# Splitting the B and C rows later, and a dense tile's gates, experts and residual a section sooner

## The reference

```python
x_ = einsum('ed,bld->bel', in_proj_w, ctx); u = silu(conv4(x_) + conv_b)
dt_lo, Bm, Cm = split(einsum('ke,bel->bkl', x_proj_w, u))          # 32, 16, 16 rows
delta = softplus(einsum('er,brl->bel', dt_proj_w, dt_lo) + dt_proj_b)
state = state * exp(delta_t * A) + (delta_t * u_t) * B_t           # per state, over time
y = (sum over states of state * C_t + D * u) * silu(z)             # z = layernorm(x)
x = x + y
```

```python
xn = layernorm(x); logits = xn @ W_router.T; h = xn @ A_w
x = x + xn @ W_base.T + b_base + sum over top-2 e of gate_e * 2 * (h_e @ B_w[e])
```

## Time and profile before

| | us |
|---|---|
| median of 3 runs (lowest, highest) | 2019.85 (2019.84, 2026.95) |
| the profiled execution, its own time | 2023.09 |
| its span | 2021.3 |
| PE, DVE, POOL, ACT busy | 1808.8, 1744.8, 1681.3, 1290.0 |
| share of PE, DVE, POOL, ACT | 89%, 86%, 83%, 64% |
| DMA | 435.01 MB, mean 215 GB/s |

### The profile page before, as it was taken

One profiled execution on the slowest core, in us unless ns is written; L12 is line 12 of the kernel. 1 busy time (PEld: TensorE's weight loads), 2 busy tenths in 40 slices (PEclk: granted clock), 3 DMA queues, 4 the chain that ended last, 5 costly groups with the idle time before them and its releaser, 6 DMA issues.

```text
span 2021.3 us, 25834 instructions
## 1 busy us (share of the span) xinstructions
PE 1808.8 (89%) x9000; PEld 1171.5 (58%) x9000; DVE 1744.8 (86%) x1397; ACT 1290.0 (64%) x1800; POOL 1681.3 (83%) x751
## 2 busy tenths in 40 slices
PE   8778888888788889899988899898999999989999
PEld 3346666666455555555555555565666666665554
DVE  3699999988999999999999999999999999995111
ACT  3485666666666676766676766666877777773332
POOL 0298999999998999999999999999999999997100
PEclk9889999998889999899999999999999999999999
DMA  4656666687786667697766676686676767666100
GB/s 160 213 199 211 218 209 205 211 298 268 240 283 215 217 201 223 219 311 256 250 221 218 205 230 212 213 299 224 233 226 225 227 227 224 226 228 246 57 31 32
DMA packets 158705, 435.01 MB, mean 215 GB/s; under 512 B 14608, under 2 KB 47632, under 8 KB 158576
## 3 DMA queue, kind: packets, MB, share of 16 engines
q1 hardware_dynamic: 155120, 420.79, 61.4%
q0 software_dynamic: 3456, 12.58, 3.2%
HBM read 382.46 MB, written 50.86 MB: 214 GB/s over the span
## 4 chain that ended last, share of the span: by engine, by line
DVE 38%; PE 31%; issue 15%; POOL 8%; ACT 6%; DMA 1%; DVEq 0%; POOLq 0%; SPq 0%; ACTq 0%
DVE state L1277 24%; DVE row L1259 9%; PE bank_a L642 6%; PE y_ps L586 6%; POOL prod L1419 5%; DVE conv L1251 3%; PE bank_b L642 3%; PE row L664 3%; POOL drive_rows L1412 2%; ACT decay L980 2%; PE row L580 2%; PE row L543 1%; PE bank_b L519 1%; PE bank_b L500 1%; ACT row L980 1%
## 5 line engine op out<-in xcount | busy, mean ns | idle before, releaser
L1419 POOL TENSOR_TENSOR prod<-state,c_rows 128x1024 f32<-128x1024 f32 x512 | 1209.5, 2393 | 101.1 <-PE y_ps L586 50.1
L1277 DVE TENSOR_TENSOR_SCAN state<-decay,row 128x1024 f32<-128x1024 f32 x355 | 808.8, 2283 | 21.0 <-PE row L580 13.5
L586 PEld LDWEIGHTS y_ps<-ident,prod 128*128 128x128 f32 x4096 | 488.0, 146 | 245.8 <-issue 158.7
L586 PE MATMUL y_ps<-ident,prod 128*128 128x128 f32 x4096 | 552.0, 282 | 46.2 <-POOL prod L1419 46.1
L642 PE MATMUL bank_a<-w_o,xnT 128*128 128x512 f32 x816 | 388.1, 606 | 12.3 <-DVE x L1324 12.3
L980 ACT ACTIVATE decay<-delta,a 128x1024 f32<-128x1024 f32 x355 | 397.3, 1137 | 1.5 <-DMA u_d<-decay 1.4
L1412 POOL TENSOR_TENSOR drive_rows<-du,b_rows 128x1024 f32<-128x1024 f32 x157 | 376.5, 2398 | 6.9 <-DMA b_rows<-bc_d 6.9
L1259 DVE TENSOR_TENSOR row<-du,row 128x1024 f32<-128x1024 f32 x296 | 358.1, 1210 | 25.1 <-PE row L543 24.8
L1277 DVE TENSOR_TENSOR_SCAN state<-row,drive_rows 128x1024 f32<-128x1024 f32 x157 | 357.3, 2276 | 19.3 <-POOL drive_rows L1412 15.5
L980 ACT ACTIVATE row<-delta,a 128x1024 f32<-128x1024 f32 x157 | 175.4, 1117 | 261.3 <-DVE state L1277 260.8
L543 PE MATMUL row<-parts,sel 96*128 96x512 bf16 x592 | 189.6, 403 | 80.7 <-DVE state L1277 74.3
(11 more groups left out here) (160 smaller groups left out, 1879.3 us busy)
## 6 DMA issues: line engine op xcount, KB each, us to landing
c_rows<-bc_d SPq DMA_DIRECT2D x512, 512.0 KB, 4.6
xrow<-in_x SPq DMA_DIRECT2D x32, 512.0 KB, 5.3
skip<-u_d SPq DMA_DIRECT2D x32, 512.0 KB, 8.8
yy_d<-yy SPq DMA_DIRECT2D x32, 512.0 KB, 6.5
u_d<-conv SPq DMA_DIRECT2D x24, 512.0 KB, 5.3
ctx<-u_d SPq DMA_DIRECT2D x48, 256.0 KB, 6.2
x<-in_x SPq DMA_DIRECT2D x24, 512.0 KB, 5.8
x<-yy_d POOLq DMA_DIRECT2D x24, 512.0 KB, 9.5
```

Source lines behind the costliest of these rows:

```text
L586: last = nc.tensor.matmul(y_ps[:, i * P:(i + 1) * P], source[:, i * P:(i + 1) * P], ident[:, :], start=(first and i % (H // P) == 0), stop ...
L1277: nc.vector.tensor_tensor_scan(state[:, q % STATES, :], factor, term, 0.0, ALU.mult, ALU.add).then_inc(scan_done, 1)
L1419: nc.gpsimd.tensor_tensor(prod[:, q % PRODS, :], state[:, q % STATES, :], c_rows[:, q % RING, :], ALU.mult).then_inc(prod_ready, 1)
```

## The change

Five things are edited. On PE `turn_gates` goes from section 11 to the end of section 10 (behind `add_up`), the experts of half 0 from section 12 to section 11, and half 1 of the product begins in section 12: in blocks without a third half two steps k in each of sections 12 to 15, in blocks with one none, three, two and three. On ACT `take_gates` goes from section 11, behind both table loads, to section 10, ahead of them. On DVE the residual of half 0 goes from section 13 to 12. On ACT the second split goes from section 7 to 9 and the third from 10 to 13. On POOL the second subtraction goes from section 8 to 10. No instruction is added or removed.

```diff
--- before.py
+++ after.py
@@ -758,15 +758,14 @@
                         k = 2 * at.index(m)
                         product(j, 0, [k, k + 1], beside, True)
                     if m == 11:
-                        turn_gates(j, beside, True)
-                    if m == 12:
                         experts(j, 0, beside)
                 for i, at in enumerate(front_plan(E)[0]):
                     if m in at and len(HALVES[E]) > i and m >= 9:
                         project(E, i, [k for k in range(NK) if at[k % len(at)] == m])
                 if dense:
-                    if m >= 13:
-                        product(j, 1, range(2 * (m - 13), NE if m == 15 else 2 * (m - 13) + 2), beside, True)
+                    if m >= 12:
+                        ks = ((), (0, 1, 2), (3, 4), (5, 6, 7)) if len(HALVES[E]) > 2 else ((0, 1), (2, 3), (4, 5), (6, 7))
+                        product(j, 1, ks[m - 12], beside, True)
                     if m == 15:
                         experts(j, 1, beside)
 
@@ -776,6 +775,8 @@
                     add_up(q - 2)
                 if m == 6:
                     add_skip(E)
+                if dense and m == 10:
+                    turn_gates(j, beside, True)
 
                 if m == 15 and E + 1 < NBLK and ON_PE[E + 1]:
                     turn_du(E + 1, 0)
@@ -1139,7 +1140,7 @@
                     take_gate(E, gate_at(E).index(m - 1))
                 if last and m - 1 in sizes_at(E):
                     take_v(E + 1, sizes_at(E).index(m - 1))
-                if last and m == 7:
+                if last and m == 9:
                     split_second(b + 1)
                 if dense and m == 5:
                     take_routing(j, beside)
@@ -1152,8 +1153,10 @@
                         gate_scale(E + 1)
                 if r == NE - 2 and b + 1 < B and m == 9:
                     take_xd(b + 1, 0)
-                if last and m == 10:
+                if last and m == 13:
                     split_third(b + 1)
+                if dense and m == 10:
+                    take_gates(j, beside)
 
                 if E + 1 < NBLK:
                     if m == 10:
@@ -1162,8 +1165,6 @@
                     if m == 11:
                         table(SILU)
                         gate_rows(E + 1)
-                if dense and m == 11:
-                    take_gates(j, beside)
                 if (E, m) in DIAGONALS_AT:
                     make_diagonal(*DIAGONALS_AT[E, m], range(NE))
                 if E == 0 and m >= FIRST_PIECE:
@@ -1367,7 +1368,7 @@
                     else:
                         dve.wait_ge(gate_copied, 2 * E + 2)
                     gates(j, beside)
-                if dense and m == 13:
+                if dense and m == 12:
                     add_residual(j, 0, beside)
                 scan(E, m)
                 if m == 2 and E:
@@ -1454,7 +1455,7 @@
                 product(E * DS + m)
                 if j >= -1 and m == 6:
                     add_yy(j + 1, E if r == 0 else E - 1)
-                if r == NE - 1 and b + 1 < B and m in (6, 8):
+                if r == NE - 1 and b + 1 < B and m in (6, 10):
                     split_rest_of(b + 1, m == 6)
                 if m == 12 and E + 1 < NBLK:
                     make_du(E + 1)
```

## The result

The forecast was 2013.2 us, 6.7 us (0.33%) under the median then shown. Measured side by side on one chip, the changed kernel takes 2030.26 us (median of 20 runs, 2023.5 to 2041.51), the kernel before 2023.3 (20 runs, 2018.73 to 2028.24). The ratio is 1.0037, 95% interval 1.0026 to 1.0049: 7.5 us slower, between 5.3 and 9.9. The direction was wrong, and by 14 us in all. (Against the 2013.2 the median lies 17 us off; 3.5 of that is the starting point, a median of three runs that twenty runs put at 2023.3.) The profiled execution took 2029.47 us, span 2027.7 (before: 2023.09 and 2021.3). The lengths of blocks (first scan to first scan) split these 6.4 us: up to the end of block 8 it is 3.4 us shorter (3.3 of it by the end of block 6, ahead of every edit, so not by the change); blocks 9 to 23 are 5.0 us longer, blocks 24 to 31 4.8 us.

What follows compares the result with a forecast made beforehand. VectorE and GpSimd, both nine tenths busy, were taken as the bound, gains lasting only if GpSimd follows. 6.7 + 2.7 - 0.7 - 2.0 = 6.7 us off 2019.85 gave 2013.2 us; range 2008 to 2021.5.

Steps and rivals of the forecast that it cites:

- part 5: TensorE leaves section 15 sooner, idles ahead of section 2's gate transposes, clock falls in five blocks: costs 2.0 us, bounds 0 to 5.
- The slower rival: TensorE's clock falls in blocks 24 to 31 behind idle time grown from 1.14 to 1.5 us: 3 us slower, 2023; chance 0.08.
- parts 2 and 3: Experts and third half moved in blocks with a third half; ScalarE's gates' copy ahead of its table loads: each valued at 0.
- Part 1: Half 1 begins a section sooner, so waits at ends of blocks 10, 13, 21 and for the residual go: 6.7 us gained.
- Part 4: Later splits and subtraction: 2.7 us gained at block 23's end, 0.7 lost in block 7, nothing in block 15.
- The rival in which nothing is removed: The residual still waits and TensorE's idle time stays: part 1 is 0, sum near 0, 2020; 0.26 shared with gains given back.
- The one with more than forecast: VectorE truly the bound in block 23 and the half-speed stretch never comes: 12.9 us gained, 2007; chance 0.14.

Runs made afterwards that it cites:

- e3: Changed kernel with half 1 of the dense product back in sections 13 to 15, earlier gates and experts kept; 1.0011 of the kernel before (2023.9 us).
- e12: Changed kernel with one matmul whose result nobody reads in section 1 of blocks 24 to 31 alone; 1.0002 of the kernel before (2024.33 us).
- e5: Kernel before plus unread filler matmuls in section 1: two in blocks 10 to 23, one in 24 to 31; ratio 0.997 (2016.74 us).
- e6: Changed kernel with the same filler matmuls as e4, but the splits at their old places; 0.9927 of the kernel before (2008.21 us).
- e4: Changed kernel plus unread filler matmuls in section 1: two in blocks 10 to 23, one in 24 to 31; 0.9927 of the kernel before (2009.03 us).
- e9: Changed kernel with half 1 back in sections 13 to 15 and the filler matmuls of e4; 0.9982 of the kernel before (2020.36 us).
- e1: Kernel before with the later splits alone (second split, third split, second subtraction); ratio 1.0011 (2026.42 us).
- e2: Changed kernel with the splits put back to their old places, no filler; 1.0031 of the kernel before (2031.89 us).
- e10: e4 with two more filler matmuls in sections 0 and 1 of block 9, splits later only in block 23; 0.992 of the kernel before (2006.91 us).
- e11: Changed kernel with filler matmuls only in blocks 11, 14, 16, 19, 22 (two) and 24 to 31 (one); 0.9991 of the kernel before (2020.2 us).

## Why the prediction was wrong

**The step that failed is part 5, the term of 2.0 us.** The mechanism was the right one and stands in the text: TensorE leaves section 15 sooner, waits longer ahead of the gate's transposes, and its clock falls. The size was wrong. After the change `drive` waits 23.0 us; before, 20.6 less the 7.8 at the four ends and 3.5 of block 23 left 9.3. So the term is 13.7 us, with 2.0 taken and 5 as its upper end; with the filler 6.4 us of waits remain. Three readings made it small:
- The price of a fall was had by dividing 9.3 us over all 15 blocks, and a block was to pay 1.0 at most. But before the change only seven blocks had a fall in section 2 or 3, with waits of 5.2 us behind it, up to 1.5 in a block; the rest of the 9.3 stands at other places. Now the five blocks counted (11, 14, 16, 19 and 22) pay 7.8 us more, 1.6 each; block 11 pays 0.79 + 1.03.
- Only those five were counted. In the seven others the idle time grew as well (2.75 and 2.50 to 2.89), and in some of them the half speed now lasts through the 16 instructions of section 3's `add_up` (3.62 us in place of 2.12 in block 12). They pay 6.0 us more: block 12's waits went from 1.19 to 2.26 us, block 18's from 0.38 to 1.90, block 21's at these places from none to 1.86.
- Blocks 24 to 31 were left at zero in the sum; the profile shows 4.8 us there.

Stretch by stretch the profile's miss of 13.1 us (6.7 sooner forecast, 6.4 later measured) is this: blocks 9 to 23 were to be 7.4 us shorter and are 5.0 longer, the rest behind them was to stay and is 4.8 longer, and ahead of them 0.7 longer was forecast and 3.4 shorter came, nearly all of it ahead of any edit, which is chance.

**The slower rival named the second place, with its chance far too low.** I gave it 0.08, since the idle time would grow from 1.14 to 1.5 us. It grew to 2.2: of the two us by which section 15 is lighter one comes back as idle time here, and I had argued only a third of a microsecond without working it out. Section 15 is not the whole of it either: with half 1 put back (e3) the gap is still 1.78, so 0.6 of the growth comes with the earlier gates and experts, whose parts 2 and 3 were put at nothing; by which of them is not shown. Per fall it costs 3.3 us and 0.6 in the next block, not 1.8, in block 28; but it comes in two blocks of seven, not in all, and the one in block 31 cost next to nothing. By e12 it is worth some 7 us on the median, with intervals that just touch.

The Trainium skill (TensorE: Matmul & The Clock Gate, section "Why this matters for your kernels") asks only to avoid idle gaps above about 3 us. In this trace the clock fell behind gaps of 2.0 to 2.9 us in a dozen blocks, and those falls decided the sign of the change; where the two differ the measurement decides.

**Part 1 was right in kind and, with the filler in place, too small:** 6.7 forecast, 8.7 (e5 to e6) or 11 (e4 to e9) measured. The stall after 2.81 us of idle time is gone, and with it every wait of `drive` at section 15; a part of the gain is in the next block's sections 1 and 2 (e9). Without the filler it is all given back, and more.

**Parts 2 and 3 were right for VectorE,** apart from the idle time of TensorE said above: outside block 23 no wait of VectorE for ScalarE's decay came up in sections 13 and 14, and blocks 25 to 27 are still 51.05 to 51.08 us.

**Part 4, forecast +2.0, is near 0** (e1: 1.0011; e4 against e6 the same). In block 23 the cover that goes is GpSimd's, as said, but the stall behind it grew from 1.25 to 4.67 us, so less is kept than the 2.7. Block 15 was put at nothing, since the subtraction would fill the wait for the C row. It did, but the product behind it starts 0.8 us later, and GpSimd has no gap up to block 16: VectorE's waits for it there are 2.88 and 1.66 in place of 0.42, against 2.86 saved. From its first scan to the second of the next block, block 7 takes 58.26 us in e2 and 58.99 in the changed kernel, block 15 60.24 and 61.48, block 23 61.74 and 60.09: +0.7 as forecast, +1.2 for 0, and -1.7 for -2.7. Between the kernel before and e1 the same three differ by -0.1, +0.3 and -1.7, so the two costs depend on when the C rows land, and the medians tell no gain.

The rival in which nothing is removed is excluded (block 13's rows). The one with more than forecast had said 2007, and e4, e6 and e10 come to 2007 to 2009 where half speed is rare. That is near by luck: its sum has 6.9 us from block 23, where VectorE still waits 4.66 us in e4, and the filler is no part of the change and gains 6 us without it.

## What to carry to other kernels

When a change makes a nearly full engine's section lighter, follow where that engine waits next: time comes back as idle time there (here one to two us for two), and if TensorE's clock falls behind it, what follows costs more than the section saved. Price such a fall per block that has one, never as a mean over all, and count it in every block whose idle time grows. A few matmuls that nobody reads, put into the gap, are a cheap test of whether a kernel's loss is the clock's, and here they turned a loss of 0.4% into a gain of 0.7%.

## What the runs showed of the hardware

- The clock falls behind gaps of 2.0 us here, and not each time: in blocks 25 to 31 of the changed kernel seven gaps of 2.2 to 2.7 us are followed by two falls, in e3 six gaps of 1.8 and one of 2.3 by one, behind a gap of 1.78; in e11 one came with gaps of 1.35 us. In blocks 10 to 31 the low clock lasted up to 10.2 us at a time.
- The spread of the time from run to run goes with it. Each run has its mean granted clock on record: over 29 runs of the kernel before the times run from 2015.55 us (clock 0.953) to 2034.23 (0.944), with a correlation of -0.76; over the twelve of e11 from 2016.65 (0.956) to 2034.26 (0.943), with -0.95.
- The kernels with the full filler spread less, 2.3 us in five runs of e6, 2.6 in six of e4, 3.3 in seven of e5 and 4.8 in six of e10; but these are few runs, and e9, with the same filler and more falls, spreads over 12 us in twelve.
